# K's stacked rows for two batches in one transfer, two pair buffers, ones rows set by GpSimd

## The chip, the cores and the metric

One core of one Trainium2 chip runs the kernel. The metric is the device time in microseconds (us). Of the kernel before there are three runs: 410.93 us median, 410.18 to 411.25.

## The reference

One transformer layer over 16 batches. x is (16, 256, 256), the context (16, 120, 256); 16 heads of 16; the feed-forward part has 768 hidden columns and integer weights.

```python
scores = jnp.einsum('bhqd,bhkd->bhqk', Q, K) * SCALE / temperature
attn = jax.nn.softmax(scores, axis=-1)
out = jnp.einsum('bhqk,bhkd->bhqd', attn, V)
x = x + xattn(layernorm(x), ctx, ctx)          # Q from x; K and V from ctx; then Wo
gate, up = x' @ wg.T, x' @ wu.T                # x' = layernorm(x)
x = x + (silu(gate) * up) @ wd.T
```

## The kernel before

Every engine has its own program, made by the same loop over steps (`steps`). A batch n starts 32 steps behind batch n - 1 (`TURN`); each operation of batch n stands at step 32 n + `LAG` + `SHIFT`, and jobs of TensorE at 32 n plus the number in `JOBS`. So these tables set the order of instructions on each engine, and no time: an instruction runs when the one before it has been issued and its semaphores have come. SyncE (SP) issues all DMAs from one queue in that order.

Precision comes from splitting: f32 values become a high part and a low part (`hi`, `lo`), and K and Q become three bf16 parts (`hi`, `mid`, `third`). K is computed for two batches at once (`k` jobs run for even n only), 120 columns each. ScalarE writes the highest part k3[:, 0] (`highest`, L510 on), VectorE the rest k_rest (`rest_of`, L639), ScalarE the middle part (`middle`, L524), GpSimd the third (L468). The parts of each head have then to stand on 96 partitions one above the other. That is done by DMA from SBUF to SBUF (`stack`, L387 to L395): six transfers of 16 rows for ks and six for qs, per batch. The highest part fills three of the six, the middle part two, the third part one. Two more rows of ks are ones (L695); the rows of qs beside them receive the negated maximum of the scores, so that the second product of ks and qs (B, L920) gives scores less their maximum. The first product (A, L910) gives the scores themselves, of which VectorE takes the maximum (negmax, L710).

ks and qs have three buffers each (`RING`). k3 exists once. So ScalarE's highest part for a new pair waits until the six transfers of both batches of the pair before have landed (ks_in), and SP waits for B of batch n - 3 before it overwrites a buffer. The names that matter below: x_tok is the input of a batch; norm1 is ScalarE's normalisation of it into xn, xn1T its transpose, with hi from ScalarE (L507) and lo from VectorE (L632); rsqrt on GpSimd (L453 to L458) gives what norm1 needs; ctxT is the context, hi from ScalarE (L584) and lo from GpSimd (L483). hid, wide_any and wide_int near the start belong to a test of the integer weights, made once.

Of the kernel before, what the change touches and what calls it, by code (L numbers as in the profile page):

```python
# [14 lines left out]
RING = 3  # L15
BATCHES = 16
TURN = 32
# [32 lines left out]
    "normT2 lo": 91, "tanh": 94, "gate": 95, "hid": 96, "hid hi": 98, "hid lo": 100, "hid lo last": 118,  # L50
    "y": 123, "store": 148,
# [15 lines left out]
    "A": {0: 5, 1: 2, 3: -1, 14: -1, 15: -1},  # L67
# [5 lines left out]
    "bias x_res": {0: -16, 1: 9, 2: 4, 3: -16, 13: 10, 14: 8, 15: -5},  # L73
# [3 lines left out]
    "exp": {0: -1, 1: -1, 13: 1},  # L77
# [36 lines left out]
    "shift lo": {1: -3, 2: 2},  # L114
# [3 lines left out]
    "store": {0: -5, 2: 9, 3: 1, 13: -4, 14: -17, 15: -12},  # L118
# [863 lines left out]
```

## Time and profile before

| | |
|---|---|
| median of 3 runs | 410.93 us |
| the profiled execution | 409.33 us, its span 407.6 us, mean granted clock 0.975 |
| TensorE matmul (PE) | 363.9 us busy, 89% of the span |
| VectorE (DVE) | 298.2 us, 73% |
| ScalarE (ACT) | 256.2 us, 63% |
| GpSimd (POOL) | 158.7 us, 39% |
| DMA queue q1 | 61696 packets, 36.99 MB, 47.4% of 16 engines' span |

The span goes from the first to the last instruction of one profiled execution. PEld is TensorE's weight load, which overlaps the matmuls; SPq is SyncE's queue of DMA issues. The granted clock is the share of TensorE's full clock that the chip allowed. L910 is line 910 of the kernel.

### The profile page before, as it was taken

To read this page: it belongs to the slowest core of one execution; us is meant where nothing else is said; L and a number is where in the kernel's file an instruction comes from. 1 tells how busy PE (TensorE), PEld (TensorE's weight loads), DVE (VectorE), ACT (ScalarE), POOL (GpSimd) and SP (SyncE) were. 2 spreads that over 40 slices of the span, in tenths; PEclk is the share of its full clock that TensorE was granted. 3 is DMA by queue.
4 is the path that set the end of the run, shared out by engine and by line. 5 is a ranking of instruction groups with operands and counts; after the bars stand their busy time and mean duration, and the time that the engine had idled before them with its cause. 6 is when DMAs were issued, how large, how long until landed. Compare 5 with 4: busy or idle time off the path is not lost.

```text
span 407.6 us, 9738 instructions
## 1 busy us (share of the span) xinstructions
PE 363.9 (89%) x3398; PEld 326.9 (80%) x3398; DVE 298.2 (73%) x734; ACT 256.2 (63%) x564; POOL 158.7 (39%) x282
## 2 busy tenths in 40 slices
PE   0567578799999999999999999999998999998984
PEld 0566465688999899989999898999997988787984
DVE  6974657678878877787788778888777686745743
ACT  2353366577776767676777686767766675756442
POOL 3133313264434443343426263626353061613322
PEclk9979689999999999999999999999999999999989
DMA  6999595536523753184525591739137622010000
GB/s 174 294 101 155 76 157 88 87 76 123 101 65 77 141 118 78 33 161 110 112 58 89 124 157 32 141 53 159 26 84 83 113 31 81 15 42 2 27 27 27
DMA packets 61749, 37.68 MB, mean 92 GB/s; under 512 B 34049, under 2 KB 61185, under 8 KB 61697
## 3 DMA queue, kind: packets, MB, share of 16 engines
q1 hardware_dynamic: 61696, 36.99, 47.4%
q8 instruction: 32, 0.52, 0.6%
q14 instruction: 21, 0.16, 0.2%
HBM read 14.04 MB, written 4.19 MB: 45 GB/s over the span
## 4 chain that ended last, share of the span: by engine, by line
PE 67%; DMA 11%; SPq 6%; DVE 5%; ACT 4%; issue 3%; POOL 3%; ACTq 0%; DVEq 0%
PE ps_w L807 28%; DMA qs<-q 9%; PE ps_w L800 9%; PE ps_o L936 6%; PE ps_b L920 6%; PE ps_a L910 6%; SPq L395 5%; PE ps_w L792 5%; PE ps_w L819 4%; PE ps_w L840 3%; DMA ks<-k 1%; ACT probs L545 1%; DVE ks L695 1%; POOL hidT L463 1%; DMA probs<-wkT 1%
## 5 line engine op out<-in xcount | busy, mean ns | idle before, releaser
L463 POOL TENSOR_TENSOR hidT<-hid,hidT 128x256 fp32r<-128x256 f32 x80 | 58.9, 738 | 124.7 <-ACT hidT L538 124.7
L807 PE MATMUL ps_w<-xn2T,wg 128*128 128x256 f32 x384 | 103.0, 301 | 0.2 <-DVE xn2T L632 0.2
L807 PE MATMUL ps_w<-xn2T,wu 128*128 128x256 f32 x384 | 96.2, 282 | 0.0
L545 ACT ACTIVATE probs<-ps_b 120x512 f32<-120x512 f32 x128 | 76.0, 593 | 22.8 <-PE ps_b L920 22.5
L710 DVE TENSOR_REDUCE negmax<-ps_a 128x4 f32<-128x480 f32 x128 | 82.8, 648 | 8.7 <-PE ps_a L910 8.4
L807 PEld LDWEIGHTS ps_w<-xn2T,wg 128*128 128x128 f32 x384 | 72.9, 190 | 1.5 <-issue 0.5
L807 PEld LDWEIGHTS ps_w<-xn2T,wu 128*128 128x128 f32 x384 | 73.1, 190 | 0.0
L910 PE MATMUL ps_a<-ks,qs 96*128 96x120 bf16 x512 | 49.9, 222 | 12.0 <-DMA qs<-q 7.5
L556 ACT ACTIVATE tanh_g<-ps_w 128x256 f32<-128x256 f32 x96 | 36.8, 383 | 37.2 <-PE ps_w L807 35.9
L807 PE MATMUL ps_w<-wd,hidT 128*128 128x256 f32 x384 | 55.8, 293 | 3.0 <-POOL hidT L463 2.6
L920 PE MATMUL ps_b<-qs,ks 98*120 98x256 bf16 x256 | 50.6, 279 | 4.6 <-ACT probs L545 3.2
L807 PEld LDWEIGHTS ps_w<-wd,hidT 128*128 128x128 f32 x384 | 48.8, 192 | 4.3 <-POOL hidT L463 3.2
L910 PEld LDWEIGHTS ps_a<-ks,qs 96*128 96x128 bf16 x512 | 31.1, 100 | 21.0 <-DMA qs<-q 9.3
L538 ACT ACTIVATE hidT<-hid 128x256 fp32r<-128x256 f32 x96 | 39.7, 414 | 12.8 <-DVE hid L772 12.0
L768 DVE SCALAR_TENSOR_TENSOR hid<-tanh_g,ps_w 128x256 f32<-128x256 f32 x96 | 39.1, 407 | 7.2 <-ACT tanh_g L556 5.4
L772 DVE TENSOR_TENSOR hid<-hid,ps_w 128x256 f32<-128x256 f32 x96 | 39.5, 411 | 1.8
L920 PEld LDWEIGHTS ps_b<-qs,ks 98*120 98x120 bf16 x256 | 26.7, 135 | 10.9 <-ACT probs L545 4.9
L936 PE MATMUL ps_o<-probs,v_one 120*32 120x256 f32 x512 | 34.3, 385 | 1.0 <-ACT probs L545 1.0
L800 PE MATMUL ps_w<-xn1T,wq 128*128 128x256 f32 x192 | 29.7, 309 | 4.6 <-DVE xn1T L632 4.6
L800 PEld LDWEIGHTS ps_w<-xn1T,wq 128*128 128x128 f32 x192 | 27.0, 211 | 5.3 <-DVE xn1T L632 4.8
L819 PE MATMUL ps_w<-ident,xn 128*128 128x128 f32 x128 | 20.5, 285 | 11.6 <-ACT xn L530 10.2
L483 POOL TENSOR_TENSOR ctxT<-ctx_raw,ctxT 128x480 fp32r<-128x480 f32 x8 | 9.7, 1212 | 46.1 <-ACT ctxT L584 46.1
(93 smaller groups left out, 602.9 us busy)
## 6 DMA issues: line engine op xcount, KB each, us to landing
qs<-q SPq DMA_DIRECT2D x96, 128.0 KB, 4.5
ks<-k SPq DMA_DIRECT2D x96, 60.0 KB, 2.6
x_tok<-x SPq DMA_DIRECT2D x16, 256.0 KB, 4.5
x_res<-x SPq DMA_DIRECT2D x16, 256.0 KB, 4.6
out<-y SPq DMA_DIRECT2D x16, 256.0 KB, 2.5
ctx_raw<-ctx SPq DMA_DIRECT2D x16, 120.0 KB, 4.3
y<-wgT SPq DMA_DIRECT2D x2, 384.0 KB, 5.7
x<-wuT SPq DMA_DIRECT2D x2, 384.0 KB, 6.7
```

What stands on the lines that cost most here:

```text
L463: nc.gpsimd.tensor_tensor(hidT[:, 1, f], hid[:, f % 2], hidT[:, 0, f].bitcast(F32), ALU.subtract).then_inc(hid_lo, 1)
L538: nc.scalar.activation(hidT[:, 0, f], hid[:, f % 2], ACT.Copy).then_inc(hi["hid"], 1)
L545: nc.scalar.activation(probs[0:NKV, e % PROBS], ps_b[0:NKV], ACT.Exp).then_inc(exp_done, 1)
L710: nc.vector.tensor_reduce(negmax[:, n % RING, qt, h0:h0 + AG], ps_a[ga % 2][:, 0:AG * NKV].rearrange("p (h k) -> p h k", h=AG), AX.X, ALU. ...
L768: nc.vector.scalar_tensor_tensor(hid[:, f % 2], tanh_g[:, f % 2], 1.0, ps[:, 0:NQ], ALU.add, ALU.mult).then_inc(gated_done, 1)
L772: nc.vector.tensor_tensor(hid[:, f % 2], hid[:, f % 2], ps[:, NQ:2 * NQ], ALU.mult).then_inc(emptied["gateup"], 1)
L800: last = nc.tensor.matmul(dst, lhsT, rhs, start=(k == 0 and one is sums[0]), stop=(k == len(one) - 1), skip_group_check=True)
L807: last = nc.tensor.matmul(dst, lhsT, rhs, start=(start and k == 0), stop=(stop and k == len(terms) - 1), skip_group_check=True)
L819: last = nc.tensor.transpose(ps[:, c * NQ + t * P:c * NQ + (t + 1) * P], src[:, t, c * P:(c + 1) * P], ident[:])
L910: last = nc.tensor.matmul(ps_a[ga % 2][:, k * NKV:(k + 1) * NKV], qs[n % RING][0:KS_ROWS, h0 + k, qt * P:(qt + 1) * P], ks[n % RING][0:KS_ ...
L920: last = nc.tensor.matmul(ps_b[0:NKV, k * NQ:(k + 1) * NQ], ks[n % RING][:, gb * HG + k], qs[n % RING][:, gb * HG + k], start=True, stop=True)
L936: last = nc.tensor.matmul(ps_o[k % HQ * VW:(k % HQ + 1) * VW, k // HQ], v_one[n % RING][:, h], probs[0:NKV, count(n, GROUPS, h // HG) % PR ...
```

## The change

ks has two buffers in place of three, each for a pair of batches: ks[n // 2 % 2] is 98 rows by 16 heads by 2 batches by 120 columns. `stack` runs for K at even n only and sends both batches of a row block in one transfer. The wait of the highest part of k is for the six transfers of the previous pair, on the semaphore of its buffer. The ones rows, three memsets of 2x1920 on VectorE before, are two of 2x3840 on GpSimd, ahead of its steps. Beside that, entries in `LAG`, `START`, `SHIFT` and the range of steps are different; what they move is shown below for two places, and lines of the tables here are only samples.

```diff
 LAG = {
-    "load ctx": -90, "load x": -90, "ctx lo": -77, "rsqrt1": -75, "ctx hi": -70, "stats1": -70, "var1": -66,
+    "load ctx": -90, "load x": -90, "ctx lo": -77, "rsqrt1": -75, "stats1": -70, "ctx hi": -69, "var1": -66,
...
-    "normT2 lo": 91, "tanh": 94, "gate": 95, "hid": 96, "hid hi": 98, "hid lo": 100, "hid lo last": 118,
-    "y": 123, "store": 148,
+    "normT2 lo": 91, "tanh": 94, "gate": 95, "hid": 96, "hid hi": 98, "hid lo": 99, "hid lo last": 118,
+    "y": 122, "store": 148,
...
+def pair_count(pair):
+
+    return (pair // 2 + 1) * (6 * 16)
...
-        ks = [sb(f"ks{r}", [KS_ROWS + 2, H, NKV], BF16) for r in range(RING)]
+        ks = [sb(f"ks{r}", [KS_ROWS + 2, H, 2, NKV], BF16) for r in range(2)]
...
-            def stack(kind, n, part, t, dst, arrived, parts):
+            def stack(kind, n, part):
 
                 at_least(sp, b_full, count(n - RING, GROUPS, GROUPS))
                 sp.wait_ge((hi, mid, lowest)[part][kind], job_count(kind, 0, n))
-                src = t[:, part, :, n % 2] if kind == "k" else t[:, part]
+                if kind == "k":
+                    dst, src, arrived, parts = ks[n // 2 % 2], k3[:, part], ks_in[n // 2 % 2], K_PARTS
+                else:
+                    dst, src, arrived, parts = qs[n % RING], q3[:, part], qs_in[n % RING], Q_PARTS
                 for r in range(len(parts)):
                     if parts[r] == part:
-                        sp.dma_start(dst[n % RING][r * D:(r + 1) * D], src).then_inc(arrived[n % RING], 16)
+                        sp.dma_start(dst[r * D:(r + 1) * D], src).then_inc(arrived, 16)
...
                 for n, part in due("k rows", i, 3):
-                    stack("k", n, part, k3, ks, ks_in, K_PARTS)
+                    if n % 2 == 0:
+                        stack("k", n, part)
...
             pool.wait_ge(consts_done, 1)
+            for pair in range(2):
+                nc.gpsimd.memset(ks[pair][KS_ROWS:], 1.0).then_inc(k_ones_set, 1)
+                pool.wait_ge(k_ones_set, pair + 1)
...
-            def highest(kind, n, t, w, bias, arrived):
-
-                for back in ((2, 1) if kind == "k" else (1,)):
-                    if n >= back:
-                        act.wait_ge(arrived[(n - back) % RING], slot_count(n - back, 1, 1) * (6 * 16))
+            def highest(kind, n, t, w, bias):
+
+                if kind == "k" and n > 0:
+                    act.wait_ge(ks_in[(n // 2 - 1) % 2], pair_count(n // 2 - 1))
+                if kind == "q" and n > 0:
+                    act.wait_ge(qs_in[(n - 1) % RING], slot_count(n - 1, 1, 1) * (6 * 16))
...
-                if i == START["ones rows"]:
-                    for r in range(RING):
-                        last = nc.vector.memset(ks[r][KS_ROWS:], 1.0)
-                    last.then_inc(k_ones_set, 1)
...
-                        pe.wait_ge(ks_in[n % RING], slot_count(n, 1, 1) * (6 * 16))
+                        pe.wait_ge(ks_in[n // 2 % 2], pair_count(n // 2))
...
-                                                ks[n % RING][0:KS_ROWS, h0 + k], start=True, stop=True)
+                                                ks[n // 2 % 2][0:KS_ROWS, h0 + k, n % 2], start=True, stop=True)
...
-                        pe.wait_ge(k_ones_set, 1)
+                        pe.wait_ge(k_ones_set, 2)
...
-                        last = nc.tensor.matmul(ps_b[0:NKV, k * NQ:(k + 1) * NQ], ks[n % RING][:, gb * HG + k], qs[n % RING][:, gb * HG + k],
+                        last = nc.tensor.matmul(ps_b[0:NKV, k * NQ:(k + 1) * NQ], ks[n // 2 % 2][:, gb * HG + k, n % 2], qs[n % RING][:, gb * HG + k],
```

SP's queue near the start, before; shapes are in elements, and the first six rows with ks or qs belong to batch 0, those behind ctx_raw to batch 1:

```order
L395 DMA ks<-k 16x16x120 x2
L395 DMA qs<-q 16x8x512 x3
L395 DMA ks<-k 16x16x120
L372 DMA ctx_raw<-ctx 128x2x120 x2
L395 DMA ks<-k 16x16x120 x3
L408 DMA bo_row<-bo 128x256
L395 DMA ks<-k 16x16x120 x2
L377 DMA x_tok<-x 128x2x256
L395 DMA ks<-k 16x16x120
L395 DMA qs<-q 16x8x512 x6
```

and the same place now:

```order
L404 DMA ks<-k 16x8x480 x2
L404 DMA qs<-q 16x8x512 x3
L404 DMA ks<-k 16x8x480
L378 DMA ctx_raw<-ctx 128x2x120 x2
L383 DMA x_tok<-x 128x2x256
L404 DMA qs<-q 16x8x512 x3
L417 DMA bo_row<-bo 128x256
L404 DMA qs<-q 16x8x512 x3
```

The six ks transfers of batch 1 are gone, x_tok of batch 3 has moved up, and bo_row stands among the qs transfers of batch 1.

VectorE around the first maxima of batch 0 (negmax) and the rest of q of batch 1 (q_rest), before:

```order
L710 TENSOR_REDUCE negmax<-ps_a 128x4
L651 BN_AGGR meanvar<-stats 128x2 x2
L639 SCALAR_TENSOR_TENSOR q_rest<-ps_w,bq_col,q 128x256 x2
L710 TENSOR_REDUCE negmax<-ps_a 128x4
L676 TENSOR_TENSOR hid<-ps_o,ident 128x128
L678 TENSOR_REDUCE wide_any<-hid 128x1
L681 TENSOR_SCALAR wide_any<-wide_any 128x1
L710 TENSOR_REDUCE negmax<-ps_a 128x4
L639 SCALAR_TENSOR_TENSOR k_rest<-ps_w,bk_col,k 128x240 x2
```

and now:

```order
L665 BN_AGGR meanvar<-stats 128x2 x2
L720 TENSOR_REDUCE negmax<-ps_a 128x4
L690 TENSOR_TENSOR hid<-ps_o,ident 128x128
L692 TENSOR_REDUCE wide_any<-hid 128x1
L695 TENSOR_SCALAR wide_any<-wide_any 128x1
L653 SCALAR_TENSOR_TENSOR q_rest<-ps_w,bq_col,q 128x256 x2
L720 TENSOR_REDUCE negmax<-ps_a 128x4 x2
L653 SCALAR_TENSOR_TENSOR k_rest<-ps_w,bk_col,k 128x240 x2
```

q_rest has moved behind the three steps of the weight test; k_rest, of the second pair, stands behind the fourth maximum as before.

VectorE at its start, before:

```order
L645 BN_STATS stats<-x_tok 128x6 x2
L651 BN_AGGR meanvar<-stats 128x2 x2
L695 MEMSET ks 2x1920 x3
L645 BN_STATS stats<-x_tok 128x6 x2
L608 RECIPROCAL temp_row<-temp_row 128x16
```

and GpSimd at its start now, where the memsets stand:

```order
L455 MEMSET eps_col 128x2
L456 MEMSET zero_col 128x2
L457 MEMSET ones_col 128x1
L460 MEMSET ks 2x3840 x2
L466 TENSOR_TENSOR minus_mean<-zero_col,meanvar 128x2
L467 TENSOR_TENSOR vareps<-meanvar,eps_col 128x2
```

The two memsets are ahead of the first rsqrt of batch 0; on VectorE nothing takes their old place, and a little later xn1T lo has moved ahead of k_rest.

## Rows read from the trace of the kernel before

**Rows 1.** Stretches: busy us (instructions) per engine, granted clock, DMA share, GB/s

```profile
0.00:33.00 33.00, 15.81 (x83) 15.14 (x84) 23.03 (x43) 12.16 (x17) 8.49 (x21) 0.90 0.87 188
33.00:50.00 17.00, 10.57 (x89) 8.90 (x89) 10.41 (x27) 5.64 (x12) 7.20 (x13) 0.80 0.75 108
50.00:61.00 11.00, 8.04 (x74) 6.29 (x73) 5.84 (x11) 6.97 (x15) 1.22 (x2) 0.84 0.99 152
97.00:118.70 21.70, 21.70 (x215) 19.90 (x214) 17.05 (x42) 15.32 (x35) 9.74 (x17) 1.00 0.39 88
162.00:183.80 21.80, 21.13 (x211) 19.17 (x209) 17.48 (x48) 15.74 (x36) 9.79 (x19) 1.00 0.50 97
```

**Rows 2.** Chain of waits, 0 to 62 us: start, us, what

```profile
32.83 5.36 DMA ks<-k
38.19 2.49 issue
40.67 0.82 ACT k L518 x2
```

**Rows 3.** Timeline, 33 to 48 us: start, us, engine, instruction [idle before <-releaser]

```profile
35.45 0.84 DVE L639 SCALAR_TENSOR_TENSOR q_rest<-ps_w,bq_col,q 128x256 f32<-128x256 f32 x2
36.77 0.28 DVE L676 TENSOR_TENSOR hid<-ps_o,ident 128x128 f32<-128x128 f32 x1
37.09 1.09 ACT L530 ACTIVATE xn<-x_tok,norm_bias,rstd 128x256 f32<-128x256 f32 x2
43.06 1.20 PE L910 MATMUL ps_a<-ks,qs 96*128 96x120 bf16 x8 [3.68 <-DVE negmax L710]
```

**Rows 4.** Timeline, 0 to 18 us

```profile
4.38 0.43 DVE L601 CAST wk<-probs 128x512 fp32r<-128x512 f32 x1 [1.90 <-DMA probs<-wkT]
6.23 0.46 SPq L377 DMA_DIRECT2D x_tok<-x  x1
6.64 0.20 POOL L453 TENSOR_TENSOR minus_mean<-zero_col,meanvar 128x2 f32<-128x2 f32 x1 [5.02 <-DVE meanvar L651]
10.06 2.90 PE L792 MATMUL ps_w<-ctxT,wk 128*128 128x240 f32 x12
10.95 1.66 DVE L695 MEMSET ks<- 2x1920 bf16 x1 [0.35 <-issue]
16.71 0.68 DVE L632 TENSOR_TENSOR xn1T<-ps_w,xn1T 128x512 fp32r<-128x512 f32 x1
```

**Rows 5.** GpSimd's groups: busy us, mean ns of one, idle before

```profile
L483 POOL TENSOR_TENSOR ctxT<-ctx_raw,ctxT 128x480 fp32r<-128x480 f32 x8 | 9.7, 1212 | 46.1 <-ACT ctxT L584 46.1
L440 POOL MEMSET ident<- 128x128 f32 x1 | 0.2, 205 | 0.3 <-POOLq L976 0.3
L976 POOL MEMSET const-float32-1.0<- 128x1 f32 x1 | 0.1, 99 | 0.0
```

**Rows 6.** DMA issues: count, KB each, median us from issue to landing

```profile
qs<-q SPq DMA_DIRECT2D x96, 128.0 KB, 4.5
ks<-k SPq DMA_DIRECT2D x96, 60.0 KB, 2.6
x_tok<-x SPq DMA_DIRECT2D x16, 256.0 KB, 4.5
```

**Rows 7.** Timeline of SP's queue, 60 to 72 us

```profile
62.57 4.40 SPq L395 DMA_DIRECT2D ks<-k  x6
67.07 4.23 SPq L395 DMA_DIRECT2D qs<-q  x6
```

**Rows 8.** Chain of waits, then TensorE's timeline, both before the scores of batch 3

```profile
70.75 5.98 DMA qs<-q
...
76.78 0.38 PE L910 MATMUL ps_a<-ks,qs 96*128 96x120 bf16 x4 [1.55 <-DMA qs<-q]
```

**Rows 9.** TensorE's timeline: the q products of batches 2 and 3

```profile
47.12 2.46 PE L800 MATMUL ps_w<-xn1T,wq 128*128 128x256 f32 x12
60.53 1.68 PE L800 MATMUL ps_w<-xn1T,wq 128*128 128x256 f32 x12
```

More of the change, by code:

```diff
@@ L59 @@
 START = {
-    "load wv": -96, "load wo": -44, "load bv": -116, "load bo": -21, "weight q": -72, "weight o": -25,
-    "weight v": -51, "ones rows": -133, "load wg": (-57, -51), "load wu": (-47, -45), "load wd": (-42, -40), "int hi": (-46, -29, -21),
-    "int lo": (-36, -25, -18), "squares": (-20, -19, -15, -14, -11, -9), "tell": -3, "sum": 2, "told": 7, "read": 63,
+    "load wv": -96, "load wo": -44, "load bv": -116, "load bo": 1, "weight q": -72, "weight o": -33,
+    "weight v": -54, "load wg": (-57, -51), "load wu": (-51, -45), "load wd": (-42, -40), "int hi": (-46, -29, -22), "int lo": (-36, -25, -18),
+    "squares": (-20, -19, -15, -14, -11, -5), "tell": -7, "sum": 2, "told": 8, "read": 63,
 }
 SHIFT = {
-    "A": {0: 5, 1: 2, 3: -1, 14: -1, 15: -1},
+    "A": {0: 5, 1: 2, 3: -1, 13: -2, 14: -1, 15: -1},
+    "B": {1: -4},
     "att": {0: -1},
@@ L72 @@
     "attT lo": {13: 2, 14: -1},
-    "bias x_res": {0: -16, 1: 9, 2: 4, 3: -16, 13: 10, 14: 8, 15: -5},
+    "bias x_res": {0: -16, 1: 5, 2: 4, 3: -16, 13: 10, 14: 8, 15: -5},
     "ctx hi": {0: -47, 1: 18, 2: 1, 13: 6, 15: 1},
@@ L76 @@
     "down": {14: -1, 15: 38},
-    "exp": {0: -1, 1: -1, 13: 1},
+    "exp": {0: -1, 1: -5, 13: 1},
     "gate": {15: 23},
@@ L113 @@
     "shift hi": {0: 8, 1: -1, 15: -1},
-    "shift lo": {1: -3, 2: 2},
+    "shift lo": {1: -3, 2: 2, 13: -1},
     "shift rows": {0: 6, 1: 4, 2: -5, 14: -6, 15: -11},
@@ L117 @@
     "stats2": {0: -3},
-    "store": {0: -5, 2: 9, 3: 1, 13: -4, 14: -17, 15: -12},
+    "store": {0: -5, 2: 9, 3: 9, 13: -4, 14: -17, 15: -12},
     "tanh": {14: 1, 15: 21},
-    "v": {0: 4, 1: -7, 2: 16, 3: 5},
-    "var1": {0: -73, 1: -11, 2: -5, 3: -9, 13: -3, 14: 1, 15: 1},
+    "v": {0: 4, 1: -7, 2: 16, 3: 5, 15: 2},
+    "var1": {0: -73, 1: -11, 2: -7, 3: -9, 13: -6, 14: 1, 15: 1},
     "var2": {0: -3, 15: 2},
     "wo": {0: -1, 3: -2},
-    "x1": {0: -3},
-    "y": {0: -1, 13: -3, 14: 3, 15: 41},
+    "x1": {0: -3, 13: -1},
+    "y": {0: -1, 13: -3, 14: 3, 15: 44},
 }
-FIRST, LAST = -222, TURN * (BATCHES - 1) + 229
+FIRST, LAST = -205, TURN * (BATCHES - 1) + 232
 @lru_cache(None)
@@ L288, in build @@
         qs_in = [sem(f"qs_in{r}") for r in range(RING)]
-        ks_in = [sem(f"ks_in{r}") for r in range(RING)]
+        ks_in = [sem(f"ks_in{r}") for r in range(2)]
         shift_in = [sem(f"shift_in{r}") for r in range(RING)]
@@ L426, in step @@
                 for n, part in due("q rows", i, 3):
-                    stack("q", n, part, q3, qs, qs_in, Q_PARTS)
+                    stack("q", n, part)
                 for n, _ in due("store", i):
@@ L547, in step @@
                     if n % 2 == 0:
-                        highest("k", n, k3.rearrange("p a c b k -> p a c (b k)"), 2 * NKV, bk_col, ks_in)
+                        highest("k", n, k3.rearrange("p a c b k -> p a c (b k)"), 2 * NKV, bk_col)
                 for n, half in due("pv copy", i, 2):
@@ L564, in step @@
                 for n, _ in due("q hi", i):
-                    highest("q", n, q3, NQ, bq_col, qs_in)
+                    highest("q", n, q3, NQ, bq_col)
                 for n, _ in due("norm2", i):
```

4 lines of the change are left out of this document (2 added, 2 removed), and 26 rows, old and new, of tables (LAG, SHIFT).

## The prediction

> **What bounds the kernel now.** I read the table of stretches first. From 97 us on TensorE is never free: 21.70 us busy of 21.70 in one turn (a turn is one batch), 21.13 of 21.80 in one of the worst [rows 1]. A turn costs what its matmuls cost, and the change takes no matmul away. TensorE's idle time lies in the first 33 us (17.2 us), between 33 and 61 us (9.4 us), in a few waits up to 80 us and in the tail. So a gain has to come from the first 80 us. The granted clock says that idleness is paid twice: it is 0.80 and 0.84 between 33 and 61 us and 1.00 later [rows 1].
>
> The chain of waits says what the start hangs on [rows 2]: a transfer of ks, issued at 32.83, of 5.36 us; then 2.49 us booked to nothing that the profile shows; then ScalarE's highest part of k at 40.67. In the code that activation waits for ks_in of the batch before, batch 1, so I read the 2.49 us as the last pieces of that transfer. The timeline shows what hangs on it: TensorE's scores of batch 0 stand 3.68 us behind negmax, and negmax stands behind k_rest in VectorE's order [rows 3].
>
> **Three memsets leave VectorE.** They are 1.66 us each, the first issued behind the statistics of batch 0, the last at 10.95, so VectorE is free of them at 12.61 [rows 4]. What is late next: the statistics of batch 1, whose x_tok is issued at 6.23 + 0.46 us and lands after 4.5 us (median) [rows 4, 6], at 11.2, or 11.5 with the weights in front of it. So VectorE wins 1.1 us, not the whole length of the memsets. Up to xn1T lo (16.71 to 17.39 [rows 4]) it then has the same work less k_rest (about 0.8 us), which now stands behind: xn1T lo ends at 15.6.
>
> **Two memsets of 2x3840 come onto GpSimd, ahead of everything.** No row shows one of that length. Nearest are the memsets of 128x128 in 205 ns and of 128x1 in 99 ns [rows 5]: 106 ns for 127 elements, 0.83 ns each, so 0.1 + 3840 x 0.83 = 3.3 us each. Lower bound: if time goes by bytes (bf16 is half of f32), 1.7 us each. Upper bound: the two-input subtract of 480 elements in 1212 ns [rows 5], (1.21 - 0.1) / 480 = 2.3 ns, 9.0 us each. I take 3.3, the same operation. Then GpSimd is free at 1.6 + 2 x 3.3 + 0.2 = 8.4 us and was needed at 6.64 [rows 4]; the norm of batch 0, ctxT lo and the k product (10.06 to 12.96 [rows 4]) come 1.7 us later. K product to 14.7, k hi to 15.5, k_rest behind xn1T lo from 15.6 to 16.4, where before it ended at 16.8. From there the order runs through k mid, the highest part of wg, q hi and q_rest on ScalarE and VectorE in turn, so the 1.8 us that the q product wins are lost behind k_rest again. I count 0.2 us for the whole start. What hides GpSimd's 1.7 us is VectorE's work up to xn1T lo. With the lower bound the gain is about 1 us; the upper bound is a rival.
>
> The Trainium skill (SBUF - State Buffer, section Who interferes with whom) speaks against this place: GpSimd shares a port pair with VectorE, and a cast in a two-port mode waits until a GpSimd instruction that started first has ended. The trace has the cast of wk at 4.38 in 0.43 us for 512 elements [rows 4], quick against the 0.86 ns per element of the ks memset, but no long GpSimd instruction beside it. It is priced as a rival.
>
> **Six transfers of ks per pair instead of twelve.** The issue order prints the new piece as 16x8x480 where q's is 16x8x512 and the old one was 16x16x120. In bf16 these are 960, 1024 and 240 bytes, so a new transfer moves 120 KB in 128 pieces; I go by this form. What goes is 48 of 96 issues of ks, of 0.6 to 0.7 us on the SP queue (4.40 for six [rows 7]). Where SP waits for others that is worth nothing, and it mostly does. Two places count.
>
> First place, batch 1: the six issues that end at 33.39 vanish, and with them the wait of k hi for them; the pair's last row block has been issued earlier, in front of them. ScalarE would run k hi right behind norm1, 37.09 to 38.18 [rows 3]: 2.5 us earlier. But the new order puts q_rest of batch 1 behind hid (36.77 [rows 3]) and the two wide_any steps behind it. They move forward with it, as one negmax less stands before them, and q_rest starts about 0.9 us later than 35.45 [rows 3], and q mid, norm1 and k hi with it: 39.1 for 40.67. That leaves 1.5 us. Next late is the transfer of qs of batch 1: its third part is ready at about 39.1, is issued at once and lands 4.5 us later (median [rows 6]), at 43.7; TensorE has to have it by its wait of before, 45.28, less 1.5. It just fits, so I take 1.5 us.
>
> Second place, batch 3: SP issues its six ks transfers from 62.57 to 66.97 and only then its qs, from 67.07 to 71.30 [rows 7]. TensorE waits 1.55 us for them at 76.78 [rows 8]. Now five of the six qs go out earlier. The last one is issued at 70.75 as before, since it waits for GpSimd's third part, and it took 5.98 us [rows 8] because the others were in front of it; with them gone the median of 4.5 is the nearest row: 75.2, when TensorE's own work ends. The 1.5 us are gained. Later odd batches give nothing: their turns have no idle time (21.70 of 21.70).
>
> The pieces themselves: the skill (DMA: Bandwidth & Descriptors, Why small descriptors are slow (HBM only)) says that transfers between SBUF and SBUF do not suffer from small pieces. By it the larger pieces buy nothing; my sum has no term for them either way.
>
> **What the pair costs.** Six qs took 4.23 us to issue, and the last landed at 76.73, 9.7 us after the first issue began. Less 2.6 us for a transfer by itself [rows 6] that is 7.1 / 6 = 1.2 us each for 128 KB, so 1.1 for a new ks and 0.55 for an old one. In even batches qs stand behind the last ks, so up to 0.6 us later, in seven batches with hardly any slack: 0 to 4.2 us. There the last ks waits for GpSimd's third part, by when the first five have drained; I take 0.3 in all. Two buffers in place of RING = 3 cost nothing: SP already waited for B of batch n - 3 before ks of an even n, and an odd n - 3 ends the pair that the new transfer overwrites.
>
> **Clock.** The 12 matmuls of a q product took 2.46 us at 47.12, after the idle stretch, and 1.68 at 60.53 [rows 9]. With 1.5 us less idle before it I take half of these 0.8 us: 0.4. The rest of the new order (y ahead of negmax, B of batch 1 earlier, the steps of batches 13 to 15) I bound by 1 us either way, which is the size of the single waits for matmul results here, and put at 0.
>
> **Sum.** -0.2 (start) - 1.5 (k hi) - 1.5 (qs of batch 3) - 0.4 (clock) + 0.3 (even batches) = -3.3 us. The profiled execution took 409.33 (span 407.6 and 1.7 around it) and becomes 406.0. The median of the runs, 410.93, is 1.6 above it; so 407.6.
>
> **Rivals.** (a) All waits of the start go: 2.5 us for k hi, 1.5 for batch 3, 1.7 for an idle piece of that size behind them, 0.8 of clock and 1 for a short memset: -7.5, 403.4. For it: 9.4 us are idle between 33 and 61 us. Against: q_rest is moved later. (b) The pair's bulk shifts qs in every even batch: +4.2 instead of +0.3, 411.5. For it: 0.67 us of idle in the turn from 162 us [rows 1] leaves no slack. Against: the pause before the last ks. (c) The port: the cast of wk waits for both memsets, from 4.38 to 8.4. The norm of batch 0 and ctxT lo then wait for the statistics behind the cast; k product 12.9 to 15.8, k_rest to 17.5, q_rest 0.8 us later than before, 1.0 lost against my sum: 408.6. (d) GpSimd's memset takes 9.0 us: GpSimd is free at 19.8 instead of 6.64, 13.2 late. The q product, before 17.5 to 20.4, can start only behind the k product at about 26, and 8.5 us are lost at the head; with 3.1 gained later, +5.4: 416.3. It decides from about 1.6 ns per element, where the loss reaches the gain. Against: the memset rows at 0.83. (e) The change does not do what it says, as a moved step opens a wait as large as those it closes: 411.
>
> **Chances.** Forecast 0.55 (its own range 405.5 to 409.5), (a) 0.13, (b) 0.09, (c) 0.08, (d) 0.10, (e) 0.05. A measurement of this kernel tells about 0.3% (1.2 us) from no change. Faster: 0.52 of the forecast, all of (a), most of (c): 0.71. Same: the rest of these, most of (b) and (e): 0.17. Slower: (d) and a little of (b) and (e): 0.12. Range 403.0 to 411.5.
>
> **What would show it.** Right: k hi of the second pair within 0.2 us of norm1's end, near 39; no wait for qs near 75; GpSimd's memsets near 3.3 us; 48 issues of ks; turns after 97 us still with under 1 us idle. Wrong: memsets of 5 us or more; a cast of wk that starts after 5 us; new waits for qs in even turns; scores of batch 0 still held up by k_rest past 42.

## Result and profile after

The changed kernel is 0.7% slower. Its median is 412.83 us (11 runs, 411.22 to 415.8) beside 410.18 us of the kernel before on the same chip; the ratio is 1.0071, 95% interval 1.0042 to 1.0100. Measured a second time it gave 1.0063 (1.0020 to 1.0106). Forecast were 407.6 us and a range of 403.0 to 411.5. The profiled execution took 414.28 us, its span 412.1.

The table of stretches of the changed kernel answers to [rows 1], with its columns; the row from 61 us is new:

```profile
0.00:33.00 33.00, 17.04 (x77) 16.36 (x78) 19.32 (x40) 12.15 (x18) 14.79 (x23) 0.84 0.90 200
33.00:50.00 17.00, 12.73 (x100) 10.92 (x98) 10.52 (x27) 5.77 (x13) 6.59 (x13) 0.70 0.67 105
50.00:61.00 11.00, 6.70 (x54) 4.36 (x52) 5.57 (x10) 5.96 (x12) 1.81 (x2) 0.81 0.94 132
61.00:76.00 15.00, 13.38 (x84) 10.57 (x85) 6.17 (x17) 6.40 (x12) 2.21 (x5) 0.57 0.24 48
97.00:118.70 21.70, 20.63 (x205) 18.76 (x204) 17.08 (x43) 15.44 (x35) 9.97 (x17) 1.00 0.53 101
162.00:183.80 21.80, 21.80 (x215) 19.93 (x214) 17.70 (x45) 15.52 (x37) 9.62 (x17) 1.00 0.39 66
```

From 33 to 50 us TensorE is busier than before, but at a clock of 0.70 where it was 0.80. Between 50 and 61 us it is busy 1.3 us less (6.70 for 8.04). Then comes a stretch at about half the clock, 0.57 on average over 15 us; the second profile of this kernel, below, does not have it.

The DMA issues answer to [rows 6]: 48 issues of ks of 120 KB, as forecast, at 4.0 us to landing for 2.6. The page of the profile counts 42496 packets on the queue for 61696, with the same 36.99 MB, and 46.6% of the 16 engines' span for 47.4%: larger pieces save next to no engine time.

```profile
qs<-q SPq DMA_DIRECT2D x96, 128.0 KB, 4.3
ks<-k SPq DMA_DIRECT2D x48, 120.0 KB, 4.0
```

The start, from the timelines of GpSimd, VectorE and TensorE (answers to [rows 4] and, for the rest of q, [rows 3]):

```profile
1.67 6.81 POOL L460 MEMSET ks<- 2x3840 bf16 x2
8.56 0.19 POOL L466 TENSOR_TENSOR minus_mean<-zero_col,meanvar 128x2 f32<-128x2 f32 x1
4.32 0.93 DVE L615 CAST wk<-probs 128x512 fp32r<-128x512 f32 x1 [1.85 <-DMA probs<-wkT]
15.28 2.90 PE L810 MATMUL ps_w<-xn1T,wq 128*128 128x256 f32 x12 [0.41 <-DVE xn1T L646]
20.48 1.27 POOL L481 TENSOR_TENSOR k<-k_rest,k 128x480 bf16<-128x480 f32 x1
20.84 1.46 DVE L617 TENSOR_TENSOR wo<-probs,wo 128x512 fp32r<-128x512 f32 x1
22.56 0.86 DVE L653 SCALAR_TENSOR_TENSOR q_rest<-ps_w,bq_col,q 128x256 f32<-128x256 f32 x2
23.48 1.11 PE L829 MATMUL ps_w<-ident,xn 128*128 128x128 f32 x4 [4.06 <-DVE q_rest L653]
34.06 0.60 PE L920 MATMUL ps_a<-ks,qs 96*128 96x120 bf16 x8
36.80 0.88 DVE L653 SCALAR_TENSOR_TENSOR q_rest<-ps_w,bq_col,q 128x256 f32<-128x256 f32 x2
38.24 1.08 ACT L544 ACTIVATE xn<-x_tok,norm_bias,rstd 128x256 f32<-128x256 f32 x2
39.23 0.79 ACT L532 ACTIVATE k<-ps_w,bk_col 128x240 bf16<-128x240 f32 x2
41.58 1.20 PE L920 MATMUL ps_a<-ks,qs 96*128 96x120 bf16 x8 [0.45 <-DVE negmax L720]
```

The memsets are as forecast, two in 6.81 us. The 12 matmuls of the q product of batch 0 start at 15.28 for 17.54, about as forecast. But the rest of q of batch 0 starts at 22.56, no earlier than before (22.20 there), since the cast and subtract of wo (the weight of the output projection) now stand ahead of it, and TensorE's transpose of xn (L829) waits 4.06 us for it. The scores of batch 0 start at 34.06 for 33.39. The highest part of k of the second pair runs at 39.23, right behind norm1 and without a wait, 1.44 us earlier than before; the wait of 3.68 us at 43.06 [rows 3] is 0.45.

TensorE's waits for qs, from its timeline (batches 1, 2, 4, 6, 8 and 14; batch 3 waits no longer). In brackets stands the idle time before the scores:

```profile
44.61 0.58 PE L920 MATMUL ps_a<-ks,qs 96*128 96x120 bf16 x4 [1.83 <-DMA qs<-q]
61.24 0.58 PE L920 MATMUL ps_a<-ks,qs 96*128 96x120 bf16 x4 [3.31 <-DMA qs<-q]
101.47 0.38 PE L920 MATMUL ps_a<-ks,qs 96*128 96x120 bf16 x4 [1.07 <-DMA qs<-q]
144.62 0.38 PE L920 MATMUL ps_a<-ks,qs 96*128 96x120 bf16 x4 [0.35 <-DMA qs<-q]
188.40 0.38 PE L920 MATMUL ps_a<-ks,qs 96*128 96x120 bf16 x4 [1.05 <-DMA qs<-q]
317.52 0.38 PE L920 MATMUL ps_a<-ks,qs 96*128 96x120 bf16 x4 [2.46 <-DMA qs<-q]
```

Batch 1's scores start 0.67 us earlier than before (44.61 for 45.28), batch 2's 1.56 later (61.24 for 59.68). So the gain of the head is gone by batch 2. All waits from there on are in even batches, where the transfers of a pair of K stand ahead of qs. They are not new: the kernel before waits for qs in the same even batches, 0.50 us in batch 4, 0.67 in batch 8 and 1.79 in batch 14. Its waits from 80 to 338 us (total us, times, longest), to set beside the 4.9 us of the change shown below:

```profile
PE ps_a L910 <- DMA qs<-q: 3.2, 4, 1.8
```

### The profile page after: what moved, and what is told of

Same layout as the page of the kernel before. It is cut to its first block, busy times and chain, and to the rows that moved or that the text cites. A ratio compares the mean times of both kernels' runs of the same rounds, so it can differ in the third digit from the quotient of the medians.

```text
span 412.1 us, 9668 instructions
## 1 busy us (share of the span) xinstructions
PE 371.4 (90%) x3398; PEld 333.1 (81%) x3398; DVE 295.8 (72%) x731; ACT 256.1 (62%) x564; POOL 164.9 (40%) x284
## 3 DMA queue, kind: packets, MB, share of 16 engines
q1 hardware_dynamic: 42496, 36.99, 46.6%
## 4 chain that ended last, share of the span: by engine, by line
PE 71%; DMA 10%; POOL 5%; ACT 4%; SPq 4%; DVE 4%; issue 2%; ACTq 0%; POOLq 0%; DVEq 0%
PE ps_w L817 28%; PE ps_w L810 9%; DMA qs<-q 8%; PE ps_o L946 7%; PE ps_b L930 6%; PE ps_a L920 6%; PE ps_w L802 6%; PE ps_w L829 4%; SPq L404 4%; PE ps_w L850 3%; POOL ks L460 2%; DMA x_res<-x 2%; ACT probs L559 1%; POOL hidT L476 1%; PE ps_o L901 1%
## 5 line engine op out<-in xcount | busy, mean ns | idle before, releaser
L920 PE MATMUL ps_a<-ks,qs 96*128 96x120 bf16 x512 | 51.1, 227 | 11.3 <-DMA qs<-q 10.1
L930 PE MATMUL ps_b<-qs,ks 98*120 98x256 bf16 x256 | 51.9, 285 | 4.4 <-ACT probs L559 4.2
L920 PEld LDWEIGHTS ps_a<-ks,qs 96*128 96x128 bf16 x512 | 32.4, 102 | 21.0 <-DMA qs<-q 11.7
L778 DVE SCALAR_TENSOR_TENSOR hid<-tanh_g,ps_w 128x256 f32<-128x256 f32 x96 | 39.1, 407 | 7.3 <-ACT tanh_g L570 4.2
L829 PE MATMUL ps_w<-ident,xn 128*128 128x128 f32 x128 | 21.2, 292 | 17.6 <-ACT xn L544 13.4
L946 PE MATMUL ps_o<-probs,v_one 120*32 120x256 f32 x512 | 35.5, 396 | 0.0
L810 PE MATMUL ps_w<-xn1T,wq 128*128 128x256 f32 x192 | 31.7, 322 | 0.6 <-DVE xn1T L646 0.6
L829 PEld LDWEIGHTS ps_w<-ident,xn 128*128 128x128 f32 x128 | 15.0, 148 | 19.6 <-issue 15.3
```

The costliest lines, as they stand in the source:

```text
L778: nc.vector.scalar_tensor_tensor(hid[:, f % 2], tanh_g[:, f % 2], 1.0, ps[:, 0:NQ], ALU.add, ALU.mult).then_inc(gated_done, 1)
L810: last = nc.tensor.matmul(dst, lhsT, rhs, start=(k == 0 and one is sums[0]), stop=(k == len(one) - 1), skip_group_check=True)
L829: last = nc.tensor.transpose(ps[:, c * NQ + t * P:c * NQ + (t + 1) * P], src[:, t, c * P:(c + 1) * P], ident[:])
L920: last = nc.tensor.matmul(ps_a[ga % 2][:, k * NKV:(k + 1) * NKV], qs[n % RING][0:KS_ROWS, h0 + k, qt * P:(qt + 1) * P], ks[n // 2 % 2][0:K ...
L930: last = nc.tensor.matmul(ps_b[0:NKV, k * NQ:(k + 1) * NQ], ks[n // 2 % 2][:, gb * HG + k, n % 2], qs[n % RING][:, gb * HG + k], start=Tru ...
L946: last = nc.tensor.matmul(ps_o[k % HQ * VW:(k % HQ + 1) * VW, k // HQ], v_one[n % RING][:, h], probs[0:NKV, count(n, GROUPS, h // HG) % PR ...
```

## The experiments

Every ratio is against the kernel before, run on the same chip. A(n) is the start of the scores of batch n in the profiled execution. One interval is about plus or minus 0.3%, so a step of 0.2 to 0.3% between two kernels is not shown by that pair alone; where several pairs have it, I take it as likely. And the profile is one execution, whose time can lie 4 us from the median.

| transfers and ones rows | old tables | new tables |
|---|---|---|
| as before, ones on VectorE | 1 | 1.0001 |
| as before, ones on GpSimd | 0.9951 | 0.9982 |
| pair buffers, a transfer per batch | 0.9975 | 1.0006 |
| pair buffers, only pair 0 merged | 0.9958 | 0.9981 |
| all pairs merged | 1.0002 | 1.0071 (the change) |

**New tables alone** (the kernel before, with the tables of the change and the ones rows still on VectorE).

> The kernel before (three ks buffers, twelve ks transfers of 60 KB per pair, ones rows on VectorE) with the changed kernel's order tables. Theory M (merged transfers): the two 120 KB transfers of the second pair (middle and third part) stand in front of the qs of batch 2, which lands 1.5 us later (61.2 for 59.6); TensorE then stands 3.3 us and runs at half clock for 13.7 us, which costs another 3 us. By M this kernel has no such transfers and stays within 1 us of before, near 410. Theory T (tables): B of batch 1 four steps earlier and q hi of batch 3 behind one more exp make the loss; by T this is about 413. Theory P (ones rows on GpSimd): near 410, as M.

Measured: 1.0001 (0.9968 to 1.0034). A(3) 76.2. The order is not a gain by itself. But its profile changes how the head is to be read: with all twelve transfers still sent, the highest part of k of the second pair runs right behind norm1, and batch 3 no longer waits for qs (76.20 for 76.78 before). ScalarE, then TensorE at batch 3:

```profile
38.84 1.08 ACT L531 ACTIVATE xn<-x_tok,norm_bias,rstd 128x256 f32<-128x256 f32 x2
39.82 0.79 ACT L519 ACTIVATE k<-ps_w,bk_col 128x240 bf16<-128x240 f32 x2
76.20 0.38 PE L911 MATMUL ps_a<-ks,qs 96*128 96x120 bf16 x4
```

**Old tables** (all of the change but `LAG`, `START`, `SHIFT`).

> The changed kernel with the order tables of before (the memsets stay on GpSimd, the ks transfers merged). M: qs of batch 2 lands near 61, TensorE waits about 3 us for it and falls to half clock: 412 to 414. T: 409 to 410, as the tables are back. P: 412 to 413.

Measured: 1.0002 (0.9964 to 1.0039), A(1) 43.1, A(2) 60.8, and there a wait of 3.5 us for qs. The same picture as in the change: early at batch 1, late at batch 2.

**Ones rows back on VectorE**

```diff
-                nc.gpsimd.memset(ks[pair][KS_ROWS:], 1.0).then_inc(k_ones_set, 1)
+                if i == -133:
+                    for pair in range(2):
+                        nc.vector.memset(ks[pair][KS_ROWS:], 1.0).then_inc(k_ones_set, 1)
```

> The changed kernel with the two memsets of the ones rows on VectorE, at the step where before had its three (two of 2x3840, about 3.3 us each). M and T: within 1 us of the changed kernel, 412 to 413.5, since the start lost nothing by GpSimd: scores of batch 0 at 34.1 against 33.4 in before. P: the k product comes 1.9 us earlier again and the whole loss of 2.7 us goes: near 410.

Measured: 1.0100 (1.0055 to 1.0145), A(0) 36.8 for 34.1. The ratio is 0.3% above the change, with intervals that overlap; the later A(0) says that GpSimd is the better place for them.

**Ones rows on GpSimd and nothing else** (three memsets of 2x1920 in the kernel before).

> The kernel before with nothing changed but the ones rows: three memsets of 2x1920 on GpSimd ahead of its steps, about 1.7 us each, in place of VectorE's three. By the prediction the start gains 0.2 us, scores of batch 0 at 33.2 to 33.6, time as before within 0.3%. If GpSimd's later start does cost, the scores of batch 0 start at 34.5 or later and the time is 0.3% up.

Measured: 0.9951 (0.9922 to 0.9981), 407.57 us; A(0) 32.7, A(1) 43.8, A(2) 58.2, A(3) 75.3. This part of the change is a gain of 0.5%, which it holds to the end. Its GpSimd and VectorE rows:

```profile
1.67 5.36 POOL L450 MEMSET ks<- 2x1920 bf16 x3
7.22 0.19 POOL L456 TENSOR_TENSOR minus_mean<-zero_col,meanvar 128x2 f32<-128x2 f32 x1 [0.19 <-DVE meanvar L654]
4.39 1.00 DVE L604 CAST wk<-probs 128x512 fp32r<-128x512 f32 x1 [1.92 <-DMA probs<-wkT]
```

Its memsets end at 7.03, when VectorE's meanvar is just ready; the two larger ones of the change end at 8.48.

**New tables with these memsets**, to close the square.

> The kernel before with the new tables and the three ones memsets of 2x1920 on GpSimd; three buffers and per-batch transfers as before. It closes a square with three kernels already measured: old tables with ones on VectorE (1), new tables with ones on VectorE (1.0001), old tables with ones on GpSimd (0.9951). Theory (the new tables take back what the ones rows gain): 1.000, 409.2 us. Rival (gains add up, and the pair buffers or the larger memsets lose it): 0.995, 407.2 us.

Measured: 0.9982 (0.9956 to 1.0008), A(0) 34.0. Between the two expectations; with the new tables the gain is smaller, and its interval holds 1.

**A transfer per batch** (the change, with the pair buffers, but 60 KB transfers at each batch's own steps; the highest part of k waits for both batches of the pair before).

```diff
-                    dst, src, arrived, parts = ks[n // 2 % 2], k3[:, part], ks_in[n // 2 % 2], K_PARTS
+                    dst, src, arrived, parts = ks[n // 2 % 2][:, :, n % 2], k3[:, part, :, n % 2], ks_in[n % 4], K_PARTS
-                    if n % 2 == 0:
-                        stack("k", n, part)
+                    stack("k", n, part)
```

> The changed kernel, pair buffers, tables and memsets as changed, but each batch sends its own six ks transfers of 60 KB in 240-byte pieces, at the steps that the tables still have for odd batches. M: the 60 KB pieces in front of qs of batch 2 are gone, it lands near 59.7, the half clock from 60 us does not come: 408.5 to 410.5; but k hi of the second pair waits again for ks of batch 1. T: 412.5 to 414, the order of the other engines is unchanged. P: 412 to 413.

Measured: 1.0006 (0.9971 to 1.0041), A(2) 59.9. The merging costs about 0.65% on top of this; the interval just misses that of the change (1.0042 to 1.0100) and overlaps that of its second measurement (1.0020 to 1.0106).

**The same with the old tables.**

> Old tables, ones rows on GpSimd (two of 2x3840), pair buffers, but every batch's ks sent by its own six transfers of 60 KB at its old steps. Beside the kernel with the new tables and the same transfers (ratio 1.0006) it gives the price of the tables alone. Theory (the tables take back what the ones rows gain, and the pair buffers cost nothing): ratio 0.996, near 407.7 us. Rival (the tables cost something only together with merged transfers): 1.000, 409.3 us. Rival (larger memsets cost what the smaller ones gain): 1.000 too, but then scores of batch 0 start at 34 us and not at 33.

Measured: 0.9975 (0.9945 to 1.0004), A(0) 33.0, A(3) 76.3. So the tables seem to cost 0.3% here too, and the step from three buffers of 2x1920 to pair buffers of 2x3840 about 0.25% in both columns.

**Only pair 0 merged**, new tables, then old tables.

```diff
+                    if n // 2 in SPLIT:
+                        dst, src = dst[:, :, n % 2], src[:, :, n % 2]
```

> The changed kernel with only the first pair's transfers merged; from batch 2 on each batch sends its own 60 KB transfers at the steps of the tables. Theory M2: merging costs twice, 1.5 us or more at qs of batch 2 (and, in some executions, a long stretch at half clock behind it), and 0.2 to 0.6 us in each later even batch, 1.6 us in all; it gains only at the first pair, where k hi no longer waits. By M2 this is 408 to 409.5, qs of batch 2 lands near 59.5. Theory B (the bytes do not matter, only that merged and new order together miss): near 412.

> Order tables of before, pair buffers, ones rows on GpSimd, and only the first pair's transfers merged. The runs so far say that the first merge gains about 1 us and each other one loses; the old tables, where q_rest of batch 1 is not behind the weight test, should let scores of batch 1 start at 43.1 (as in the kernel of e2) instead of 45.3. If these add up, qs of batch 2 lands near 58.5 and this is 407.5 to 409, faster than before by 0.3 to 0.6%. If A(1) is not what the later start hangs on (qs of batch 2 is), it is the same as before, 409.5 to 410.

Measured: 0.9981 (0.9951 to 1.0010) and 0.9958 (0.9927 to 0.9988). Merging pair 0 seems to be worth 0.2% in both columns, each step inside the intervals. With the old tables it ends the wait of the highest part of k for ks (1.98 us with a transfer per batch, none here); with the new tables there is no such wait in either kernel, and where its 0.2% comes from is not shown. From the first of these kernels to the change (1.0042 to 1.0100) the intervals are apart: merging the pairs 1 to 7 is what makes it slow. The long pieces of the chain that leads to the scores of batch 2, in the change and then here with only pair 0 merged (start, us, what):

```profile
40.25 6.52 DMA x_res<-x
46.84 1.42 POOL x_res L502 x2
49.61 1.06 POOL k L481
50.68 0.55 SPq L404
54.51 6.68 DMA qs<-q
61.24 0.58 PE ps_a L920 x4
```

```profile
40.67 5.63 DMA x_res<-x
46.37 1.42 POOL x_res L514 x2
49.15 1.06 POOL k L493
50.23 0.57 SPq L416
54.09 5.62 DMA qs<-q
```

The steps are the same. GpSimd's third part of K stands behind the bias of x_res, the last transfer of ks behind that, and six issues of qs behind that on SP. Two pieces are longer: the transfer of x_res, in front of three ks transfers of double size (6.52 for 5.63), and that of qs, behind them (6.68 for 5.62). That is 0.89 + 1.06 = 1.95 us; the start was 0.42 us earlier, and the scores of batch 2 come 1.5 us later (61.24 for 59.75).

One pair of profiles does not carry this far. The same pieces in the second profile of the change:

```profile
41.09 5.62 DMA x_res<-x
54.47 5.91 DMA qs<-q
60.43 0.39 PE ps_a L920 x4
```

Over all profiles (the one with halves, below, left out) the last qs of batch 2 takes 5.8 to 6.9 us in the nine with pair 1 merged (mean 6.3), and 5.1 to 5.6 us in nine of the ten with it sent per batch, 6.5 in the tenth (mean 5.5). So the merging makes this transfer 0.8 us longer on average. That of x_res takes 5.5 to 7.4 us in the nine and 4.3 to 6.9 in the ten: that the merging lengthens it is not shown.

**All pairs merged but pair 1.**

> The changed kernel with all pairs merged but the second (batches 2 and 3). M2: qs of batch 2 lands near 59.5 and the loss there goes, the 1.6 us of the later even batches stay: 410 to 411.5, between the kernel of e5 and the changed one. If the later merges cost nothing it is as e5.

Measured: 1.0033 (1.0005 to 1.0062), A(2) 60.2. By the medians the loss of the merging divides: pairs 2 to 7 cost 0.5% (0.9981 to 1.0033), pair 1 0.35%. The intervals of neighbours overlap, so the sum of 0.9% is shown and the division is not. This profile's last qs of batch 2 is the one of 6.5 us, though its instructions up to there are those of the kernel with only pair 0 merged (5.62): two executions can differ by that much. In the profiles with the new tables (one entry of START apart at most) the stretch from A(3) to A(12) takes 191.0, 191.0 and 191.9 us in the three kernels with pair buffers whose pairs 2 to 7 are sent per batch, 191.7 and 191.9 in the two with three buffers, and 192.0 to 192.7 in the seven profiles with these pairs merged. TensorE's waits for qs between 80 and 338 us, in the change and then with only pair 0 merged (us in total, times, longest):

```profile
PE ps_a L920 <- DMA qs<-q: 4.9, 4, 2.5
```

```profile
PE ps_a L935 <- DMA qs<-q: 3.2, 3, 2.1
```

They are 1.7 us more. The other profiles, that with halves left out, say the same of these waits: 4.0 to 5.2 us in the ten with pairs 2 to 7 merged, 2.8 to 3.8 in the nine with them sent per batch, the kernel before among these (3.2). The means are 1.3 us apart: the loss of the stretch, seen as waits.

**Each merged transfer as two of 60 KB at the same place**

```diff
+                        for b in range(2):
+                            sp.dma_start(dst[r * D:(r + 1) * D, :, b], src[:, :, b]).then_inc(arrived, 16)
```

> The changed kernel where each merged transfer of 120 KB is sent as two of 60 KB (one per batch, 240-byte pieces) directly behind one another, at the same place: the same bytes ahead of qs, twice the issues. If the cost is the bytes ahead of qs (M2), qs of batch 2 lands as in the changed kernel, 61 to 61.5, or later because SP needs three more issues of 0.6 us: 412 to 415. If it is the form of the 120 KB transfer, the landing comes back to 59.7 and the time to 410.

Measured: 1.0343 (1.0293 to 1.0394). TensorE's waits for qs over the whole span:

```profile
PE ps_a L923 <- DMA qs<-q: 14.9, 7, 3.0
```

The bytes ahead of qs are those of the change, the issues are six more for a pair, some 4 us on SP, and the waits for qs are 4.8 us more (10.1 in the change). So issues on SP do cost, in even turns; the change leaves their number there as it was and doubles the bytes. The run misses both expectations by 8 us or more. As the issues changed with it, it can't tell the bytes from the form of the merged transfers, whose packets are of 960 bytes for 240. The packets themselves speak for the bytes: those of ks take 553 us of engine time in the change and 526 before, for the same bytes in all, so a transfer of 120 KB takes 2.1 times what one of 60 KB takes.

**28 spare matmuls before the scores of batch 2**, to fill TensorE's wait.

```diff
+                        for m in range(28):
+                            nc.tensor.matmul(ps_a[0][:, m % AG * NKV:(m % AG + 1) * NKV], qs[(n - 1) % RING][0:KS_ROWS, m % H, 0:P],
```

> The changed kernel with 28 spare matmuls (a repeat of scores of batch 1, overwritten later) on TensorE in the idle time before the scores of batch 2, so that TensorE is busy for about 2.8 of the 3.3 us there; the output is not changed by them. If the half clock from 60 to 74 us follows from this idle time and is what makes most of the loss, it goes and the time falls by 2 to 3 us, to 410. If that stretch belongs to the one profiled execution only and the loss is the late landings, 412 to 413.

Measured: 1.0118 (1.0071 to 1.0165). The spare matmuls ran from 57.3 to 58.9 us and the scores of batch 2 started at 61.0, so 2 us of the wait were left. The stretch from 61 us ran at 0.89 in its profile, but the kernel is not faster.

**The change again**, unaltered.

> The changed kernel once more. Its ratio should come back, 1.004 to 1.010. The profile of it that was taken first has a half-clock stretch of 13.7 us from 60.2 us on. The kernels of e5 and e6 have the same instructions up to 80 us, and only one of them shows that stretch, so I take it for a matter of the execution: here it may be absent, and then scores of batch 3 start near 78.5 to 79 instead of 81.4 and the span is 1.5 to 3 us shorter. If it belongs to the program, it is there again.

Measured: 1.0063 (1.0020 to 1.0106), 413.88 us. Its profiled execution took 409.74 us, and its row from 61 us reads:

```profile
61.00:76.00 15.00, 12.93 (x133) 10.49 (x132) 9.74 (x26) 9.52 (x19) 4.91 (x8) 1.00 0.37 78
```

The same kernel, the same stretch: 133 matmul instructions at a clock of 1.00 here, 84 at 0.57 in the first profile. So the half-clock stretch belongs to an execution, and the spare matmuls say nothing on it, since the kernel without them can be free of it as well. This execution had its slow stretch earlier: from 50 to 61 us its clock was 0.63, where it was 0.81 in the first, TensorE was busy for 8.76 us of the 11 (6.70 in the first), and the wait for qs of batch 2 was 1.33 us for 3.31.

**The weight test back behind the rest of q of batch 1** (`"tell": -3` for -7).

> The changed kernel with one number changed: the weight test on VectorE (tell) back to its old step, so that q_rest of batch 1 stands ahead of it as before. If the moved q_rest costs what the rows say (0.9 us at q_rest), the third part of q, k hi and the scores of batch 1 come 1 to 1.5 us earlier (43.1 to 43.6 for 44.6) and the time falls by 1 us, to 411.5 to 412. If it is hidden, 412.8 as the changed kernel.

Measured: 1.0063 (1.0032 to 1.0095). A(1) is 43.9, but A(2) 61.7, behind a wait of 4.4 us: qs of batch 2 is the limit that follows, and hides it.

**One half of the tables old**: `SHIFT`, then `LAG` and `START`, all pairs merged.

> The changed kernel with the old SHIFT table, but the new LAG and START. All pairs merged. The old and new tables as a whole differ by 0.7% with merged transfers (ratios 1.0002 and 1.0071). Theory (the loss is in SHIFT, which holds the early B of batch 1 and the later norm1, normT1 hi and k jobs of batch 0): 1.001, 409.7 us. Rival (it is in LAG and START, which hold the later weight test of q_rest and the int parts): 1.006, 411.7 us.

> The changed kernel with the old LAG and START, but the new SHIFT. All pairs merged. Theory (the loss is in SHIFT): 1.006, 411.7 us. Rival (it is in LAG and START): 1.001, 409.7 us. If both this kernel and the one with the old SHIFT come out at 1.003 or more, no single table holds the loss.

Measured: 1.0086 (1.0046 to 1.0127) and 1.0028 (0.9997 to 1.0059). I had put the loss in SHIFT; by the medians the larger part of it is in LAG and START (0.4% of the 0.7), though the interval of the second overlaps that of the change.

**One entry put back: wo behind the rest of q of batch 0**, in the change and in the kernel with only pair 0 merged. Nothing else moves on any engine.

```diff
-    "load wv": -96, "load wo": -44, "load bv": -116, "load bo": 1, "weight q": -72, "weight o": -33,
+    "load wv": -96, "load wo": -44, "load bv": -116, "load bo": 1, "weight q": -72, "weight o": -25,
```

> The changed kernel with one entry put back: the cast and subtract of wo stand behind the rest of q of batch 0 on VectorE again (weight o at -25, not -33). Nothing else moves on any engine. In the profile of the changed kernel the two take 0.4 and 1.46 us ahead of v_one and q_rest, and TensorE's transpose waits 4.06 us for q_rest. Theory (this entry is what the new tables cost near the start): q_rest of batch 0 starts near 20.7 instead of 22.56, the scores of batch 0 near 33.2 instead of 34.1, ratio 1.004, 411 us. Rival (the wait moves on, as scores of batch 2 wait for the transfer of qs in either case): scores of batch 0 are earlier, but the ratio stays at 1.006 or 1.007.

> The same entry put back in the kernel that has only the first pair's transfers merged and the others per batch (0.9981 so far, and 0.9958 with all tables old). Theory: the entry is worth about 1 us here too, since the transfer of qs of batch 2 comes earlier: 0.996, 407.7 us. Rival: 0.998 as before, then the loss of the tables lies elsewhere.

Measured: 1.0047 (1.0020 to 1.0075) and 0.9930 (0.9899 to 0.9961). The second is 407.60 us and the lowest ratio of all, 0.7% faster than the kernel before. The start of the first of the two, on VectorE and TensorE:

```profile
20.73 0.87 DVE L653 SCALAR_TENSOR_TENSOR q_rest<-ps_w,bq_col,q 128x256 f32<-128x256 f32 x2
21.51 0.42 DVE L615 CAST wo<-probs 128x512 fp32r<-128x512 f32 x1
21.96 0.69 DVE L617 TENSOR_TENSOR wo<-probs,wo 128x512 fp32r<-128x512 f32 x1
21.86 1.09 PE L829 MATMUL ps_w<-ident,xn 128*128 128x128 f32 x4 [3.10 <-ACT xn L544]
32.24 0.58 PE L920 MATMUL ps_a<-ks,qs 96*128 96x120 bf16 x8
```

The rest of q starts 1.83 us earlier, the transpose 1.62, the scores of batch 0 1.82 (34.06 to 32.24). The other kernel has A(0) 32.4; the eight profiles with the new tables, pair buffers and memsets on GpSimd, but without this entry put back, have 33.7 to 34.9. The ratio falls by 0.2% in the change, where qs of batch 2 takes part of it, and by 0.5% where the later pairs are not merged; in both pairs the intervals overlap, in the second by little (0.9951 to 1.0010 and 0.9899 to 0.9961). Between these two last kernels, alike but for the merging of pairs 1 to 7, the intervals are clearly apart: 1.2%. With the old tables the same merging costs 0.4% (0.9958 to 1.0002).

## Why the prediction was wrong

**The step that failed is "What the pair costs".** The prediction put 0.3 us on seven even batches and kept 4.2 as a bound. The runs show 0.5% for pairs 2 to 7 (2.1 us) and 0.35% for pair 1 (1.4 us): 3.5 us with these tables, near the bound, 4.8 us with wo put back and 1.8 with the old tables. The mechanism was worked out, with 1.1 us for a new transfer and 0.55 for an old one; then it was priced away with "by when the first five have drained". Two things were wrong in that. First, the pause is too short in three of the seven pairs. In pair 1 SP issues the last three ks transfers at 47.75 to 51.23 and six qs directly behind, 51.27 to 55.10; the sixth ks is issued at 50.68, and the fifth lands at 51.70. In pairs 2 and 6 the fifth lands 1.7 and 3.9 us after the issue of the sixth; in pairs 3, 4 and 5 it is 0.2 to 0.3 us, and only in pair 7 has it landed before. Second, a drained queue does not make the cost go away: the wait of batch 14, of pair 7, is 2.46 us in the change for 1.79 before and 2.1 to 2.2 in the five kernels with the new tables and the later pairs per batch. There was nothing for the delay to hide in, since the kernel before already waited for qs in these even batches, 3.2 us between 80 and 338; the prediction took them as having little slack and did not list their waits. Rival (b) named this mechanism, with a chance of 0.09. Its sign, "new waits for qs in even turns", came as longer waits in the same turns.

The steps of the table add up to the result, from the kernel before by way of the new tables: memsets on GpSimd -0.5%, tables +0.3, pair buffers with the longer memsets +0.25, pair 0 merged -0.25, pairs 1 to 7 merged +0.9. Only the first and the last are clear of their intervals.

**"The start, -0.2" had the wrong sign.** The steps up to the q product were right: product at 15.28 (forecast 1.8 us earlier than 17.54, measured 2.26; 1.6 in the second profile), memsets 3.30 and 3.47 us each (forecast 3.3). The prediction then said that the gain is lost behind the rest of k and ScalarE's weight. It was lost to VectorE's cast and subtract of wo, which `START` had moved ahead of the rest of q of batch 0, and scores of batch 0 came 0.7 us later (1.3 in the second profile), not 0.2 earlier. Putting them back brings A(0) 1.8 us forward and the ratio down by 0.2 to 0.5%. The entry was in the tables and in the order; the prediction listed only the rows at VectorE's start and around the first maxima. The 0.5% that the ones rows gain on their own (0.9951), for which the prediction had 0.2 us, were taken back so: 0.3% by the tables, in which this entry is the one found, and 0.25% by pair buffers and longer memsets together.

**"First place, batch 1, -1.5" was right as an event, and less than half of it came as a time.** The highest part of k starts at 39.23 for a forecast of 39.1, right behind norm1. The scores of batch 1 are 0.67 us earlier, and those of batch 2 are held by qs. The cause was not the one given, or not it alone: with the new tables and all twelve transfers it runs right behind norm1 as well, so that it came out as forecast is in part luck. The merging of pair 0 is worth 0.2%, 0.7 to 1.0 us, by two pairs of kernels, neither clear of its intervals.

**"Second place, batch 3, -1.5" came, but the new order alone gives it.** No wait for qs near 76 to 81. The 1.5 us were gained after 1.56 had been lost at batch 2. With the new tables alone this wait is gone too, with the six ks transfers of batch 3 still sent; with the old tables and only pair 0 merged it is there (0.97 us).

**"Clock, -0.4" did not come.** From 33 to 50 us the clock was 0.70 for 0.80. The q product of batch 2, which I had taken at less than 2.46 us, ran in 2.91 in both profiles of the change.

**The port, rival (c), acts but is small here.** The cast of wk did start at 4.32 and took 0.93 us for 0.43 [rows 4]; it ended at 5.25, just behind the first memset (4.97), and not behind both, so half a microsecond was lost, and not the 4 from 4.38 to 8.4.

**What stays open.** Which share of the loss is in the half-clock stretch past 58 us: 10 us or more of it in all lie in the first profile of the change and in four of the ten other profiles with the later pairs merged (its own repetition among the ten, and not among the four), but also in one of the nine with the later pairs sent per batch (only pair 0 merged, wo put back); the runs without a profile show no stretches. Whether it is the bytes of a merged transfer or its piece size that delays qs: no kernel changes one without the other or without more issues. What the pair buffers cost by themselves (0.25%) is not told from the longer memsets, which end 1.45 us later. And why the old SHIFT with the new LAG and START is no better than the change (1.0086): wo stands ahead of the rest of q there too, but its subtract takes 0.69 us and A(0) is 33.1, so the start is not the reason.

## What to carry to other kernels

Merging transfers for two batches halves the issues, but puts the bytes of the second batch in front of what the first batch waits for: look at what is issued directly behind, and merge only where nothing urgent follows (pair 0 here). Where an engine already waits for what stands behind, the delay has nothing to hide in; list these waits before a cost bounded from 0 to 4 us is taken near 0. A gain that a change of order and a change of transfers could both give is credited only after a run of the order alone. When tables move many instructions, go through every row that stands newly ahead of one that another engine waits for: one entry cost at least as much here as the main idea gained.

## What was not expected of the hardware

- A subtract on VectorE with both inputs in SBUF took 1.46 us (wo, 128x512) while GpSimd's third part of k, started 0.36 us before it, ran for 1.27; put back behind the rest of q it took 0.69, and so it did in its early place where that third part started later (21.57, with the old SHIFT). The Trainium skill (SBUF - State Buffer, section Who interferes with whom) says that a VectorE instruction with two SBUF inputs contends with a GpSimd one that reads SBUF, and that the one issued first holds the ports; this trace agrees, with 0.69 and 1.46.
- Beside a memset on GpSimd, which reads nothing, VectorE's cast took 0.93 us for 0.43 (1.00 beside the shorter memsets); in both it ended 0.28 us behind the memset that was running when it began. The same section has casts among those that can take the shared ports; the trace agrees.
- GpSimd sets ones in bf16 at 0.86 to 0.93 ns per element of a row (3.30 and 3.47 us for 3840, 5.36 for three of 1920). VectorE's rows read alike (3.26 us for 3840), but its two stood 4.01 us apart where GpSimd's stood 3.35 apart: the two took 7.27 us from end to end there and 6.81 here.
- Executions of one kernel on one chip differ by up to 7 us (408.38 to 415.55 for the change), and its two profiles, taken in two measurements, by 5 us at the scores of batch 3 (81.42 and 76.2), with the clock at 0.57 and 1.00 from 61 to 76 us.
- Pieces of 960 bytes in place of 240 bought next to nothing in SBUF-to-SBUF transfers: the 6144 packets of ks took 553 us of engine time, the 24576 before 526.
